# Routed rows of a mixture-of-experts layer added to three tables in memory, with five shared pairs first and three last

## The reference

```python
scores = jax.nn.sigmoid(logits) + gate_b
weights, indices = jax.lax.top_k(scores, TOP_K)
weights = weights / weights.sum(-1, keepdims=True)
shared_out = jax.nn.silu(x @ w1_shared) * (x @ w3_shared) @ w2_shared
...
h3 = jax.nn.silu(h1 * h2)
experts_out = jnp.einsum('btec,ecd->bted', h3, w2_routed)
routed_out = jnp.einsum('bted,bte->btd', experts_out, router_probs)
return shared_out + routed_out
...
x = _layernorm(x + _L0_ffn_ref(...), axis=-1)
```

## Time and profile before

| | |
|---|---|
| median of 3 runs | 547.13 us |
| lowest, highest | 545.03, 549.05 us |
| profiled execution | 546.37 us |
| its span, first to last instruction | 544.6 us |
| mean granted TensorE clock | 0.996 |
| busy in the span: PE, DVE, ACT, POOL | 95%, 79%, 68%, 53% |

### The profile page before, as it was taken

How to read it: one execution, slowest core, us unless ns; L and a number is a source line. 1 busy time by engine, 2 the same in 40 slices (tenths; PEclk the granted TensorE clock), 3 DMA queues, 4 the chain that set the end, 5 groups by cost and what they waited for, 6 DMA issues and landing times.

```text
span 544.6 us, 12215 instructions
## 1 busy us (share of the span) xinstructions
PE 519.8 (95%) x3796; PEld 362.6 (67%) x3796; DVE 431.9 (79%) x1126; ACT 372.5 (68%) x841; POOL 290.4 (53%) x336
## 2 busy tenths in 40 slices
PE   7899999999999999989999998899999999999895
PEld 4555554644454555444433387799999999999874
DVE  2489998888889999979993178987788787887685
ACT  2357778577887788969699666466767676667544
POOL 5214243122674667476868755577654554545292
PEclk9999999999999999989999999999999999999999
DMA  5964760400041625620232351477544334341495
GB/s 151 181 72 63 171 196 1 90 0 21 1 82 62 112 72 144 169 99 22 89 124 69 105 176 38 135 243 237 171 129 137 114 119 122 110 126 46 164 416 193
DMA packets 53710, 64.96 MB, mean 119 GB/s; under 512 B 8091, under 2 KB 47406, under 8 KB 53648
## 3 DMA queue, kind: packets, MB, share of 16 engines
q1 hardware_dynamic: 45968, 46.45, 32.0%
q0 software_dynamic: 7056, 17.60, 9.2%
q10 hardware_dynamic: 624, 0.13, 0.1%
HBM read 32.49 MB, written 25.62 MB: 107 GB/s over the span
## 4 chain that ended last, share of the span: by engine, by line
PE 62%; DVE 20%; POOL 8%; issue 4%; ACT 3%; DMA 1%; SPq 1%; POOLq 0%; DVEq 0%; ACTq 0%
PE psH L1705 14%; DVE MX L1161 8%; PE psO L1491 8%; PE psS L1506 7%; PE psT L1476 7%; PE psS L1568 3%; PE psX L1673 3%; PE psG L1716 3%; POOL xs_scratch L766 2%; PE psS L1511 2%; PE psY L1729 2%; PE psY L1733 2%; PE psY L1730 2%; PE psY L1732 2%; PE psY L1731 2%
## 5 line engine op out<-in xcount | busy, mean ns | idle before, releaser
L885 ACT ACTIVATE prob<-psT 128x512 f32<-128x512 f32 (+3 forms) x384 | 166.5, 496 | 37.7 <-PE psT L1476 35.5
L1161 DVE TENSOR_REDUCE MX<-psS 128x1 f32<-128x512 f32 (+3 forms) x344 | 181.9, 594 | 9.4 <-PE psS L1506 4.6
L1506 PE MATMUL psS<-KS,QS 96*128 96x512 bf16 (+3 forms) x384 | 110.2, 329 | 3.6 <-DVE MX L1161 1.6
L839 POOL DMA_INDIRECT y_scratch<-ys,dst x79 | 77.1, 976 | 65.5 <-ACT ys L1040 50.6
L1476 PE MATMUL psT<-QS,KS 98*128 98x512 bf16 (+3 forms) x384 | 107.5, 327 | 1.0 <-ACT prob L885 0.6
L766 POOL DMA_INDIRECT xs_scratch<-x1row,slotu x64 | 64.6, 1010 | 39.7 <-DVE slotu L1243 24.5
L1705 PE MATMUL psH<-wU,xh 128*128 (+1 forms) x380 | 80.9, 334 | 0.5 <-DVE z L1313 0.4
L1491 PE MATMUL psO<-prob,V 128*32 128x512 f32 (+3 forms) x768 | 76.9, 496 | 3.4 <-POOL prob L795 3.2
L795 POOL TENSOR_SCALAR_AFFINE_SELECT prob<-prob 128x512 f32<-128x512 f32 x64 | 41.6, 652 | 62.7 <-ACT prob L885 62.4
L1476 PEld LDWEIGHTS psT<-QS,KS 98*128 98x128 bf16 x384 | 34.5, 98 | 48.7 <-ACT prob L885 26.7
L1705 PEld LDWEIGHTS psH<-wU,xh 128*128 128x128 f32 x380 | 61.8, 189 | 1.2 <-issue 1.1
(11 more groups left out here) (260 smaller groups left out, 1001.5 us busy)
## 6 DMA issues: line engine op xcount, KB each, us to landing
xs<-xs_scratch SPq DMA_DIRECT2D x80, 134.0 KB
y<-y_scratch SPq DMA_DIRECT2D x16, 512.0 KB, 10.0
QS<-qp SPq DMA_DIRECT2D x48, 128.0 KB, 4.3
wU_raw<-in_L_ffn_w_routed_dram SPq DMA_DIRECT2D x32, 176.0 KB, 3.3
xs_scratch<-padrow SPq DMA_DIRECT2D x1, 2144.0 KB
xs_scratch<-padrow SPq DMA_DIRECT2D x16, 134.0 KB
x1row<-in_L_attn_x_dram SPq DMA_DIRECT2D x4, 512.0 KB, 5.6
out_dram<-x1row SPq DMA_DIRECT2D x7, 256.0 KB, 2.8
```

The source lines that it names most:

```text
L839: nc.gpsimd.indirect_dma_start(y4_dram, bass.IndirectOffsetOnAxis(ap=dst[:, n % NSEL, t:t + 1], axis=0), ys[:, n % NYS, t, :], None, bound ...
L885: nc.scalar.activation(prob[:, step % NPROB, h, 0:HALF - c0], ps[:, 0:HALF - c0], ACT.Exp).then_inc(s_Tfree, 1)
L1161: found = nc.vector.tensor_reduce(out=MX[:, c0 // HALF, heads[0]:heads[-1] + 1, i - TH * q], in_=src, op=ALU.max, axis=AX_X)
L1506: last = mm(ps[:, e * dist:e * dist + cols], QS[0:ROWS, QAT[(k // 2) % NSLOT], g % 2 * G + h, (i - TH * q) * P:(i - TH * q + 1) * P], KS[b ...
```

## The change

Three tables lie interleaved in memory, with a row for each token and 128 more for padding in each. Table 0 is filled with x1 (after the shared expert for the five early pairs, before it for the others) by seven stores of SP; tables 1 and 2 and the padding rows of table 0 are filled with zeros by 11 stores of SP in the attention stage, one behind each mask row of head groups 3 to 13. Every send now adds its 128 rows to one of the tables, j % 3 turn by turn, and waits until the write three before has landed, since the same token can be in both. Padding rows are added to the 128 spare rows. At the end 3 rows a token are read, not 4, and x1 is among them.

EARLY becomes 5. For the last three shared pairs down writes into the banks where the sums are made and leaves the sum open; PE adds the three rows of each token there. Their factor 0.5 goes into DVE's product. The ten early tiles are summed by POOL alone, two additions each. The ring ys grows from two pairs to three. Of the last quarter's scatters ten come first, and the other six follow sends 1, 3, 5, 7, 9 and 11.

```diff
-EARLY = 4
+EARLY = 5
...
+NTAB = 3
+ROWS_EARLY = [(n, t) for n in range(EARLY) for t in range(2)]
+ROWS_LATE = [(n, t) for n in range(EARLY, NSHP) for t in range(2)]
+TURN = (0, 5, 1, 2, 6, 3, 7, 4)
+GATHER = [(n, t) for n in TURN for t in range(2)]
...
-NXS, NYS, NSEL = 3, 2, 6
-NSCAT = 8
+NROW = P + B * T
+NXS, NYS, NSEL = 3, 3, 6
+NSCAT = 10
+ZCHUNK = 4
...
+ZEROED = [(k, m) for k in range(1, NTAB) for m in range(0, NROW // P, ZCHUNK)] + [(0, 0)]
+ZFIRST = 3
...
+        def landed(j):
+
+            return s_ysc[j % (2 * NTAB)], 16 * (j // (2 * NTAB) + 1)
...
+                    if ZFIRST <= k < ZFIRST + len(ZEROED):
+                        zero_rows(*ZEROED[k - ZFIRST])
...
+            def zero_rows(k, m0):
+
+                m1 = 1 if k == 0 else min(m0 + ZCHUNK, NROW // P)
+                sp.wait_ge(s_const, CONSTS)
+                sp.dma_start(tab_rows[:, m0:m1, k, :],
+                             padrow[:, 0:C].unsqueeze(1).to_broadcast([P, m1 - m0, C])).then_inc(s_zero, 16)
+
+            def store_rows(i0, tiles):
+
+                sp.dma_start(tab_rows[:, 1 + i0:1 + i0 + tiles, 0, :], x1[:, i0:i0 + tiles, :]).then_inc(s_xtab, 16)
...
+                if n == 2:
+                    sp.wait_ge(s_x1, NT)
+                    store_rows(NT - TH, TH)
+                if 2 <= n < 2 + EARLY:
+                    sp.wait_ge(s_y0, n - 1)
+                    sp.wait_ge(s_y1, n - 1)
+                    store_rows(2 * (n - 2), 2)
...
-            for i in range(NYS):
-                sp.wait_ge(s_ysc[i], 16 * len([n for n in range(MOST) if n // 2 % NYS == i]))
-            y4_rows = y4_dram.rearrange("(i p k) c -> p i (k c)", p=P, k=TOPK)
-            for i in GATHER:
-                sp.dma_start(y4[:, i, :, :].rearrange("p k c -> p (k c)"), y4_rows[:, i, :]).then_inc((s_y4a, s_y4b)[i % 2][i // 2], 16)
+            for j in range(MOST - 2 * NTAB, MOST):
+                sp.wait_ge(*landed(j))
+            for n, t in GATHER:
+                i = 2 * n + t
+                sp.dma_start(y3[:, i, :, :], tab_rows[:, 1 + i, :, :]).then_inc((s_y3a, s_y3b)[t][n], 16)
...
                 for t, s in enumerate((s_y0, s_y1)):
-                    if 2 * n + t == MOST:
+                    j = 2 * n + t
+                    if j == MOST:
                         return
                     pool.wait_ge(s, EARLY + n + 1)
+                    if j == 0:
+                        pool.wait_ge(s_zero, 16 * len(ZEROED))
+                    if j == 2:
+                        pool.wait_ge(s_xtab, 16 * (2 + EARLY))
+                    if j >= NTAB:
+
+                        pool.wait_ge(*landed(j - NTAB))
                     nc.gpsimd.indirect_dma_start(
-                        y4_dram, bass.IndirectOffsetOnAxis(ap=dst[:, n % NSEL, t:t + 1], axis=0),
-                        ys[:, n % NYS, t, :], None, bounds_check=FAR - 1, oob_is_err=False).then_inc(s_ysc[n % NYS], 16)
+                        tab_dram, bass.IndirectOffsetOnAxis(ap=dst[:, n % NSEL, t:t + 1], axis=0),
+                        ys[:, n % NYS, t, :], None, element_offset=(j + 1) % NTAB * C, bounds_check=NROW * NTAB - NTAB,
+                        oob_is_err=True, compute_op=ALU.add).then_inc(s_ysc[j % (2 * NTAB)], 16)
 
             for n in range(NSCAT):
                 scatter_rows(B - 1, NHALF - 1, n)
             for n in range(NRP):
                 send(n)
-                if NSCAT + n < TH * TOPK:
-                    scatter_rows(B - 1, NHALF - 1, NSCAT + n)
+                if n % 2 and NSCAT + n // 2 < TH * TOPK:
+                    scatter_rows(B - 1, NHALF - 1, NSCAT + n // 2)
 
             def token_rows(n, t):
 
                 i = 2 * n + t
-                pool.wait_ge((s_y4a, s_y4b)[t][n], 16)
-                link(nc.gpsimd.tensor_tensor(y4[:, i, 0:2, :], y4[:, i, 0:2, :], y4[:, i, 2:4, :], ALU.add))
-                link(nc.gpsimd.tensor_tensor(y4[:, i, 0, :], y4[:, i, 0, :], y4[:, i, 1, :], ALU.add))
...
+                pool.wait_ge((s_y3a, s_y3b)[t][n], 16)
+                link(nc.gpsimd.tensor_tensor(y3[:, i, 0, :], y3[:, i, 0, :], y3[:, i, 1, :], ALU.add))
+                nc.gpsimd.tensor_tensor(x1[:, i, :], y3[:, i, 0, :], y3[:, i, 2, :], ALU.add).then_inc(s_added, 1)
...
-                    act.wait_ge(s_ysc[n % NYS], 32 * (n // NYS))
+                    for t in range(2):
+                        act.wait_ge(*landed(2 * (n - NYS) + t))
...
+                    to = sum_bank(shared_pair(m), t) if m > LASTR else psY[:, t, 0:C]
...
+                    last = mm(to, gl[:, j, t, 1, :], wB[:, e, :], start=False, stop=(m <= LASTR))
                 last.then_inc(s_down, 1)
 
             def token_rows(n, t):
 
-                pe.wait_ge((s_y4a, s_y4b)[t][n], 16)
-                mm(sum_bank(n, t), ident[:, :], x1[:, 2 * n + t, :], start=True, stop=False)
-                for k in range(TOPK):
-                    last = mm(sum_bank(n, t), ident[:, :], y4[:, 2 * n + t, k, :], start=False, stop=(k == TOPK - 1))
+                pe.wait_ge((s_y3a, s_y3b)[t][n], 16)
+                for k in range(NTAB):
+                    last = mm(sum_bank(n, t), ident[:, :], y3[:, 2 * n + t, k, :], start=False, stop=(k == NTAB - 1))
                 last.then_inc(s_sum, 1)
```

## The result

| | before | after |
|---|---|---|
| median, us | 547.06 | 568.39 |
| lowest, highest, us | 545.03, 549.05 | 564.79, 573.11 |
| profiled execution, us | 546.37 | 565.68 |
| its span, us | 544.6 | 563.6 |
| mean granted TensorE clock | 0.996 | 0.973 |

The changed kernel takes 1.0395 times as long (95% interval 1.0296 to 1.0494). That is slower, 17 us above the prediction and outside its range. The two profiled executions differ by 19.0 us of span, and those are the ones taken apart here. Of the four executions of after, two took 5 to 7 us more than the profiled one (571.1 and 573.1), at a granted clock of 0.963 and 0.966; no profile says where.

What follows compares the result with a forecast made beforehand. TensorE was taken to bound the routed stage, busy 138.00 of 138.00 us. Terms 0 + 0 + 7 + 0 - 3 = +4 us on 546.37 gave 550.4, then 551 us against the median; bounds 548 to 556, wider range 543 to 561.

Steps and rivals of the forecast that it cites:

- Parts 1 and 2: Attention stage and early pairs: zero and x1 stores hidden, 0 to +2 us; fifth shared pair 0, bounds -1.1 to +0.7.
- Part 3: Routed stage: TensorE stops once for the rows of routed pair 16, behind the last scatter; +7 us, bounds 5.9 to 9.0.
- 3.5 + 0.75 + 0.5 + 2.1: After the last scatter: 3.5 us to SP's release, 0.75 reading row numbers and issuing, 0.5 second load's issue, 2.1 landing.
- the start, 405.2 us: When POOL issues the last scatter, 1.28 us after its second write at 403.90; PE wants the rows at 405.12.
- rival (a): Routed stage: adding in memory becomes the bound, landing over 6.0 us or dear descriptors on POOL; 578 us at 7; chance 0.22.
- Part 4: Routed stage: adding writes take L = 4.0 us from issue to landing, hidden while L is under 5.3 us; 0 us.
- a landing near 3 us: Adding write in the routed stage, estimated from the skill's rule: well under 1 us more than a plain write's 2.1.
- Part 5: Tail: reads start later but are a quarter smaller, last sum near 536.3 instead of 539.06; -3 us, bounds -5 to -1.
- Rival (b): Routed stage: the wait ahead of routed pair 16 costs nothing, through an unseen cover; 544 us, chance 0.13.
- rival (c): Neither wait comes and the smaller reads end the tail 7 us earlier instead of 3; 540 us, chance 0.08.
- its signature, pairs wider throughout: Routed stage: sign of rival (a), starts of pairs more than 4.00 us apart throughout, before and after the stop.

Runs made afterwards that it cites:

- the versions above: Three versions of the changed kernel with last-quarter scatters sooner: twelve first, rest after sends 0 to 3; all sixteen first; twelve first, rest after sends 1, 3, 5, 7: 553.56, 554.1, 551.96 us.
- schedule alone: Kernel before, plain writes, with only the scatter order changed: ten first, the other six after sends 1, 3, 5, 7, 9 and 11; 558.15 us, ratio 1.0201.
- the experiment with the nearer wait: The third version with each send waiting for the write two before instead of three; 597.47 us, ratio 1.0885.
- the third version: Changed kernel with twelve last-quarter scatters first instead of ten, and one after each of sends 1, 3, 5 and 7; 551.96 us, ratio 1.0066.

## Why the prediction was wrong

**Parts 1 and 2, zeros, stores and the fifth shared pair (0 us): about right.** Pair 0 opens at 310.9 us after and 310.7 before, pair 9 at 357.7 and 357.1. Another 0.6 us come up to pair 20, most of them at pair 19, which opens 4.5 us after pair 18: ahead of it DVE's match waited 1.1 us for a landing, the way seen in the versions above. In the page's groups PE's first waits in attention stay small:

```profile
L1544 PE MATMUL psS<-KS,QS 96*128 96x512 bf16 (+3 forms) x384 | 109.7, 327 | 4.2 <-DMA QS<-qp 1.9
```

**Part 3, the last scatters (+7 us): right in its place and its chain, wrong in one term, and that decided.** From the last scatter to PE's transposes the working gave 3.5 + 0.75 + 0.5 + 2.1 = 6.85 us; measured are 418.83 - 411.80 = 7.03 us. That these agree is partly luck: SP was released after 2.55 us, not 3.5, and issued 0.5 us later, not 0.75, but the load took 4.0 us to the transposes, not 2.6. The wrong term is the start, 405.2 us, made with the send of 0.98 us on POOL from the earlier trace rows. The prediction did ask what a dearer send would do, but only in rival (a), and only against a steady pair: two sends in 4.0 us, with a threshold of 1.7 us. At 1.54 us that threshold isn't reached, and from pair 22 on PE waits for nothing. In the stretch with six scatters in between, the room is smaller: 4 * (d + 0.30) + 1.3 has to stay under 8.0 us, so d under 1.37 us. The measured d lies between the two thresholds. That put the last scatter at 411.8 us, 6.6 us late: 5.2 by the price of the sends, and 1.4 that the working lacked with plain writes too (406.62). PE wanted its rows at 406.8 instead of 405.1, and the stop is 12.1 us instead of 6.9. With plain writes in the same kernel the stop was 6.17 us.

The second miss of this part is what follows a stop. The working counted idle time alone. After it, at a granted clock of 0.59, 0.66 and 0.58 over that pair alone, the next pair took 6.5, 5.8 and 6.5 us instead of 4.00 (after, plain writes, schedule alone): 1.8 to 2.5 us on top, and in after pairs 20 to 22 lost 15.0 us in all. These clocks lie between the levels of 1.2 and 2.4 GHz (0.5 and 1.0), so part of the pair ran at the lower; before the fall PE had stood still for 6 to 12 us. In the version with sixteen scatters first, 2.8 us of standing still were followed by the same; after waits of 1.0 us and less, with twelve first and one after each of sends 0 to 3, the clock stayed at 1.00.

**Part 4, adding in memory (L = 4.0 us, 0 in the stage): right, the 4.0 by luck.** Issue to landing is 4.0 us (3.7 to 5.4) and pairs 22 to 47 take 98.7 us, as before. No row had shown an addition; the working took 2.5 + 1.5 us between bounds of 2.1 and 8.1, and that it met the measured value is chance. That an L under 5.3 us costs the stage nothing is borne out. The restart of 0.8 us after a landing was not counted; 4.0 + 0.8 still fits, as the experiment with the nearer wait shows from the other side. The Trainium skill, "Collectives: The Full Stack", section "The bandwidth ceiling: the fold count and why AG ≠ RS ≠ AR", says of the adding step of a large collective that the addition itself is free and that two source reads halve the rate. The trace doesn't agree with half the rate for these small writes. From 440 to 509 us the software queue carries them alone (packets, MB, share of 16 engines), first with additions (the third version), then without (the same with plain writes):

```profile
q0 software_dynamic: 5146, 4.70, 56.4%
```
```profile
q0 software_dynamic: 1669, 4.55, 18.0%
```

For the same bytes that is three times the share, not twice; the share of all queues doubles, 0.39 to 0.78, because the loads beside them hardly change. Nor does the trace agree with what the prediction's estimate made of the rule, a landing near 3 us, for it is 4.0 against 2.4; and the rule is silent on the price that mattered, 1.54 against 0.97 us on POOL.

**Part 5, the tail (-3 us): wrong, +2.7.** Counted from pair 47's transposes, with the prediction's own figures beside it:

| us after pair 47 | before | predicted | after |
|---|---|---|---|
| last send | 0.1 | 4.05 | 5.8 |
| first read | 2.2 | 8.1 | 9.6 |
| last read landed | 26.7 | 27.2 | 30.3 |
| last sum | 31.3 | 28.5 | 32.4 |
| end of the span | 36.8 | 34.0 | 39.5 |

The last sends come 1.85 us apart instead of 1.28, so the reads start 1.5 us late: again the duration of a send. The reads take 20.7 us instead of 19.1. The last two tiles land 1.0 us apart, but POOL takes 1.5 for each, and so ends 2.1 us after the last landing, not 1.3. That makes 3.9 us at the last sum. POOL had waited for tiles 10.1 us in four waits: the pace of the reads, not POOL's work, set most of this stretch. The other 1.6 us are the wait at the end of the program, which the prediction took as unchanged. The prediction had the last tile's arrival and the end of POOL's other work nearly even (535.0 and 535.3 us); its last sum, 535.0 + 1.6, is 536.6 and not the 536.3 that it wrote.

**The sum.** Predicted +4, measured +19.0 us of span. The 15.0 between are 5.1 for the longer stop (12.1 against +7), 2.9 around it (2.5 of them the slow pair behind it), 1.2 up to pair 20, 0.1 in the stage and 5.7 in the tail (+2.7 against -3). Rival (b), that the wait costs nothing, and rival (c), the faster tail, are refuted. Rival (a) comes nearest to the time but not to the mechanism: its signature, pairs wider throughout, is absent. Its descriptors were the right suspect, at the wrong place.

## What to carry to other kernels

When an operation on a queue may get dearer, work out its threshold in the tightest stretch of that queue, where other work is put in between, and not only at the steady pace; then follow what the last item of that stretch releases. A late producer is best found by moving one item earlier in the order: here 12 for 10 took back 16 us. And price a stop of TensorE as these runs show it: the idle time plus some 2 us of slow clock, seen here behind each of four stops of 2.8 to 12 us.

## What the runs showed of the hardware

- An indirect write of 128 rows of 1 KB that adds occupies POOL for 1543 to 1544 ns, a plain one for 972 to 976. The software queue of the third version moved the same bytes in about twice the packets, with additions and without (packets, MB, share of 16 engines):

```profile
q0 software_dynamic: 14640, 19.56, 20.6%
```
```profile
q0 software_dynamic: 7056, 19.56, 10.0%
```

  The difference is 7584 packets, 96 for each of the 79 writes.
- The additions double the DMA share of the routed stage (0.39 to 0.78). In the profiled executions the one load that PE waited for took 4.0 us with them and 3.2 and 3.0 without (the changed kernel with plain writes, the schedule alone).
- A send that waits for a landing starts about 0.8 us after it.
- The wait between SP and PE at the end of the program varied from 0.5 to 3.5 us between kernels whose work was nearly the same.
